# Six warm-up products instead of two, the first four softmax biases on VectorE, and one rounding moved on ScalarE

## The reference

```
h    = groupnorm(x, 32 groups) * gamma + beta          # x: 4 x 128 x 32 x 32
qkv  = w_qkv @ h + b_qkv                                # q, k, v: 128 x 1024 each
attn = softmax(q.T @ k / sqrt(128))                     # 1024 x 1024
out  = x + w_proj @ (attn @ v.T).T + b_proj
```

## Time and profile before

| | |
|---|---|
| median of 3 runs | 128.53 us (128.05 to 128.63) |
| profiled execution, its own time | 128.79 us |
| span of its trace | 126.9 us |
| PE busy | 115.3 us (91%), 1187 matmuls |
| DVE, ACT, POOL busy | 94.1, 91.8, 87.3 us |
| mean granted TensorE clock | 0.973 of full |

### The profile page before, as it was taken

The page is one execution under the profiler, slowest core; times in us unless marked ns, Lnnn a source line. Parts: engine busy times, 40 slices in busy tenths (PEclk is TensorE's granted clock), DMA queues, the critical chain, the costliest instruction groups (busy, mean ns, idle before and its releaser), DMA issues.

```text
span 126.9 us, 3214 instructions
## 1 busy us (share of the span) xinstructions
PE 115.3 (91%) x1187; PEld 79.3 (62%) x1187; DVE 94.1 (74%) x237; ACT 91.8 (72%) x130; POOL 87.3 (69%) x73
## 2 busy tenths in 40 slices
PE   5976979689999999999999999999999999998981
PEld 2351346357675677667656786776568867777970
DVE  3687389788866967998569588775796887776832
ACT  3026279999989787887877878878878788788200
POOL 2054119888999998999758997999666665766000
PEclk9995599999999999999999999999999999999999
DMA  2584003699999999999999999999999999999602
GB/s 88 161 327 169 0 0 67 127 110 209 188 97 168 196 184 124 222 222 185 195 184 201 187 106 291 195 140 204 213 173 120 213 229 138 205 188 229 166 5 83
DMA packets 67727, 20.66 MB, mean 163 GB/s; under 512 B 65408, under 2 KB 66176, under 8 KB 67712
## 3 DMA queue, kind: packets, MB, share of 16 engines
q1 hardware_dynamic: 67280, 20.46, 88.9%
q10 hardware_dynamic: 432, 0.00, 0.2%
HBM read 2.36 MB, written 2.10 MB: 35 GB/s over the span
## 4 chain that ended last, share of the span: by engine, by line
PE 69%; ACT 10%; DVE 7%; DMA 7%; issue 3%; POOL 1%; SPq 0%; POOLq 0%
PE scores L754 11%; PE o_ps L772 10%; PE scores L756 10%; PE scores L755 10%; PE o_ps L780 9%; PE o_ps L773 9%; ACT probs L435 4%; DMA ptT<-p_hl 4%; DMA x_sb<-in_x_dram 3%; DVE row_max L550 3%; ACT p_hl L442 2%; PE o_ps L793 2%; DVE t_lo L538 2%; ACT z_hi L408 1%; PE misc L728 1%
## 5 line engine op out<-in xcount | busy, mean ns | idle before, releaser
L344 POOL TENSOR_TENSOR p_hl<-probs,p_hl 128x1024 f16<-128x1024 f32 x31 | 66.0, 2132 | 14.5 <-ACT p_hl L442 14.3
L550 DVE TENSOR_REDUCE row_max<-scores 128x1 f32<-128x1024 f32 x32 | 39.1, 1222 | 18.3 <-PE scores L756 18.2
L435 ACT ACTIVATE probs<-scores,exp_bias,esc 128x1024 f32<-128x1024 f32 x32 | 38.5, 1202 | 14.3 <-DVE exp_bias L555 14.2
L442 ACT ACTIVATE p_hl<-probs 128x1024 f16<-128x1024 f32 x32 | 33.8, 1057 | 1.0
L772 PE MATMUL o_ps<-v_hi,ptT 128*128 128x128 f16 x256 | 32.0, 219 | 1.7 <-issue 1.3
L773 PE MATMUL o_ps<-v_lo,ptT 128*128 128x128 f16 x256 | 32.0, 219 | 0.0
L772 PEld LDWEIGHTS o_ps<-v_hi,ptT 128*128 128x128 f16 x256 | 24.9, 98 | 8.2 <-issue 5.9
L754 PE MATMUL scores<-z_hi,t_hi 128*128 128x512 f16 x64 | 24.8, 387 | 2.9 <-ACT probs L435 2.4
L773 PEld LDWEIGHTS o_ps<-v_lo,ptT 128*128 128x128 f16 x256 | 25.0, 98 | 2.3
L755 PE MATMUL scores<-z_lo,t_hi 128*128 128x512 f16 x64 | 24.8, 387 | 0.0
L756 PE MATMUL scores<-z_hi,t_lo 128*128 128x512 f16 x64 | 24.8, 387 | 0.0
(11 more groups left out here) (136 smaller groups left out, 140.2 us busy)
## 6 DMA issues: line engine op xcount, KB each, us to landing
out_dram<-out_sb SPq DMA_DIRECT2D x7, 256.0 KB, 2.6
x_sb<-in_x_dram SPq DMA_DIRECT2D x3, 512.0 KB, 4.8
ptT<-p_hl SPq DMA_TRANSPOSE x61, 3.5
x_sb<-in_x_dram SPq DMA_DIRECT2D x2, 256.0 KB, 3.3
out_dram<-out_sb SPq DMA_DIRECT2D x1, 192.0 KB, 2.0
wqkv_sb<-in_L_conv_w_qkv_dram SPq DMA_DIRECT2D x1, 128.0 KB, 3.8
wp_sb<-in_L_conv_w_proj_dram SPq DMA_DIRECT2D x1, 64.0 KB, 3.5
wqkv_sb<-in_L_conv_w_qkv_dram SPq DMA_DIRECT2D x1, 64.0 KB, 3.2
```

Source lines behind the costliest of these rows:

```text
L344: nc.gpsimd.tensor_tensor(p_hl[:, g % RING, 1], probs[:, g % RING], p_hl[:, g % RING, 0], ALU.subtract).then_inc(plo_ready, 1)
L435: nc.scalar.activation(probs[:, g % RING], scores[:, g % SLOTS], ACT.Exp, bias=exp_bias[:, g:g + 1], scale=esc[:], accum_out=row_sum[:, g: ...
L442: nc.scalar.activation(p_hl[:, g % RING, 0], probs[:, g % RING], ACT.Copy).then_inc(phi_ready, 1)
L550: nc.vector.tensor_reduce(row_max[:, g:g + 1], scores[:, g % SLOTS], AX_X, ALU.max).then_inc(max_ready, 1)
```

## The change

```diff
-THIRD_WARM = 1
-WARM_UP = 2
+THIRD_WARM = 3
+WARM_UP = 6
...
-        bias_c = sb("bias_c", [P, 1])
...
-            pool.wait_ge(half_ready, 2)
+            pool.wait_ge(half_ready, 1)
...
             def exponentials(g):
                 if g == 0:
                     act.wait_ge(esc_ready, 2)
-                    act.wait_ge(half_ready, 2)
-
-                if g < LAG:
-                    act.wait_ge(max_ready, g + 1)
-                    nc.scalar.activation(exp_bias[:, g:g + 1], row_max[:, g:g + 1], ACT.Identity, bias=bias_c[:],
-                                         scale=neg_esc[:]).then_inc(bias_first, 1)
-                    act.wait_ge(bias_first, g + 1)
-                else:
-                    act.wait_ge(bias_ready, g - LAG + 1)
+                act.wait_ge(bias_ready, g + 1)
...
             z_high(0, 0)
-            z_high(0, 1)
             act.wait_ge(ainv_ready, 1)
             act.wait_ge(araw_ready, 1)
             nc.scalar.activation(a_hi[:], a_raw[:], ACT.Copy, scale=a_inv[:]).then_inc(ahi_ready, 1)
+            z_high(0, 1)
...
-            nc.vector.memset(bias_c[:], LOG2_P * math.log(2.0)).then_inc(half_ready, 1)
...
-                if g >= LAG:
-                    dve.wait_ge(max_ready, g + 1)
+                dve.wait_ge(max_ready, g + 1)
+                if g == 0:
                     dve.wait_ge(esc_ready, 2)
-                    nc.vector.tensor_scalar(exp_bias[:, g:g + 1], row_max[:, g:g + 1], neg_esc[:],
-                                            LOG2_P * math.log(2.0), ALU.mult, ALU.add).then_inc(bias_ready, 1)
+                nc.vector.tensor_scalar(exp_bias[:, g:g + 1], row_max[:, g:g + 1], neg_esc[:],
+                                        LOG2_P * math.log(2.0), ALU.mult, ALU.add).then_inc(bias_ready, 1)
```

More of the change, by code:

```diff
@@ L214, in attention_block @@
         max_ready = sem("max_ready")
-        bias_first = sem("bias_first")
         bias_ready = sem("bias_ready")
```

## The result

The changed kernel takes 128.59 us in the median of 18 executions, the kernel before 128.53 us of 18: by the medians there is no difference. The forecast was 126.8 us, range 125.6 to 128.4: the median lies outside it.

The account below looks back on a forecast made before the run. The chain ran on PE, on ACT alone from 16.48 to 28.5, then on PE. Exponential 3 earlier gave 128.79 - 1.75 = 127.04; the profiled execution being 0.26 above the median, the forecast was 126.8 us, range 125.6 to 128.4.

Parts of the forecast that it names:

- tile 3's: Tile 3's exponential on ACT, after a wait for POOL's `nmr`: 25.45 instead of 27.23, 1.75 us earlier.
- the forecast's own course of the clock: PE's clock falls at about 9.1 us and is back when tile 0's scores start, instead of at 15.9; chance 0.36.
- bias sum: First four biases moved from ACT to DVE: 0.41 us gained per tile where ACT sets the pace.
- Rival C: DVE becomes the bound in tiles 1 to 3 through its own work: some 0.5 us later, 127.3 us; chance 0.12.
- A: Rival: PE's clock never falls, T starts at 11.2, tile 3's exponential 2.65 us earlier, total 125.9 us; chance 0.20.
- D: Rival: products of nothing queue on PE at 1.2 GHz, T 0.85 us late, exponential 0 at 18.45, 129.4 us; chance 0.12.
- cover of the third place: PE's wait for DVE before L825 hides the third place's added products: no cost, or 0.3 us at half speed.
- A's rounding: `a_hi` moved ahead of the second half of `z_hi`: T could start 0.28 us earlier where nothing else holds it.

Follow-up runs that it names:

- the second profile: The changed kernel run again without any edit: median 128.26 us, ratio 0.9938 to the kernel before; the profiled execution took 128.28 us.
- the products alone: The kernel before with only products of nothing added, 3 in the third place and 6 in the last: 127.38 us, ratio 0.9886.
- the cold start: The changed kernel with 1 product of nothing at the start instead of 6 and none instead of 3 in the second place: 129.23 us, ratio 1.0043.

## Why the prediction was wrong

- **The step that failed** is tile 3's: "these hang on W's maximum and come 1.0 earlier, 19.25; two of 2.13 with the hand-over ... bring tile 1's to 21.45 instead of 22.62, and `nmr` to 24.65". In the forecast's own course of the clock (the second profile) the two `p_low` started at 18.7 and 20.9, even earlier than that, but `nmr` ended at 25.74. I followed POOL's queue to `nmr` and not the other thing that `nmr` waits for, `var_eps` on DVE, and on DVE's way to it stood the cast, whose 0.21 us held only in POOL's pause. Exponential 3 came at 26.57 instead of 25.45: 1.1 late, of which the cast is 1.5 and an earlier start of everything else -0.4. With the cast out of the way and the clock in the same course, exponential 3 starts at 25.28 and the execution takes 126.86 us; I had forecast 25.45 and 126.8. So the rest of the sum held, and 1.5 us of GpSimd's hold on one cast was the term it lacked.
- **The bias sum** was right per tile. From exponential to exponential I had 2.68, 3.25 and 3.25 us; with the cast moved they are 2.56, 3.24 and 3.32. Exponential 1 waited for DVE's bias as predicted, only less (0.27 behind ACT's pace of 2.28, not 0.4). Alone, with the cast in its old place, the biases were a loss all the same, 1.0044.
- **Rival C** had the right engine and the wrong cause and size: DVE was late by 1.5 us, not 0.5, and not by its own work but by one instruction that waited.
- **The clock.** I took one course as likeliest. Two are seen in profiles of the changed kernel: no fall before T (A, the profile of 127.29) and a fall and an early return (the forecast). A third, low from the start until past A's maximum, is seen in the profiles of the products alone and of the cold start, and only in the latter does it last long enough for D's queue. If the slowest group is of that kind, it had eight of 18 executions where I gave D 0.12, and this is the second reason why the median lies so high. A's price of 125.9 is what the kernel takes in that course once the cast is moved (125.8 and 125.9). D's start of T was right (12.35 summed, 12.43 with the cold start), but its price for the rest was too high: the clock was back at tile 0's scores even after a cold start, so exponential 0 started at 16.68 and not at 18.45. The execution still took 129.09 against my 129.4, but only because the cast added its 1.5 us: that agreement is luck. Before the return at 15.9 PE had worked without a gap since 11.48, 4.4 us and not the three that I wrote. In the slowest group the kernel with the cast moved takes 128.0 us, and the kernel before seems to have such a group too: its executions with a recorded mean clock of 0.996 to 1.0 lie almost all at 129.0 to 129.5, those with 0.973 mostly at 128.0 to 128.9.
- **The trace's clock** misled me at one point. I read 1.00 in the first microseconds as full. Six products from 1.37 on took 0.43 us each, so the record seems to hold 1.00 until its first event, and a clock that was low from the start cannot be seen in it, only in the lengths of the matmuls.
- **The cover of the third place** was right at full clock (0.81 us, L825's counterpart waited 0.20 for DVE) and gone at the low clock, where it starts straight behind the products, about 0.2 us late in the second profile and 0.4 with the cold start, priced at 0.3.
- **Hidden as said:** A's rounding, 0.3 us alone, and nothing where the six products run at the low clock.

## What to carry to other kernels

When an edit shifts work in time, look at every plain copy or cast of VectorE whose ends both lie in SBUF, and at what GpSimd is doing then: its duration in the old trace holds only for its old neighbour (0.21 us became 1.82 here), and a constant that is needed much later should be built before GpSimd is busy. Follow each operand of the instruction that you expect to be late next, not only its engine's queue. Judge warm-up products by the length of single matmuls over many executions, for the clock takes several courses in the same kernel and one profile shows one of them.

## What the runs showed of the hardware

- A 128x128 cast, float32 to float16, of VectorE: 0.21 or 0.22 us alone, or started 0.07 us before a GpSimd subtraction of 128x1024 ended; 1.82 us when started 0.4 us into such a subtraction of 2.13 us, in four profiles, ending with it. The same work as a `tensor_reduce` at that place: 0.27 us. `bn_stats` from SBUF beside the same subtraction took its usual 0.67 us.
- A granted clock recorded as 1.00 before its first event, while 512-column matmuls stood 0.43 us apart (the length at 1.2 GHz), up to about 12 us in the kernel with a cold start.
- Near the end SP issues transposes back to back, mostly 1.2 to 1.5 us each and now and then 2.0 to 2.3, and the last one lands 4.7 to 5.2 us later; from the last exponential to the end the profiles have between 12.0 and 12.8 us.
